# A decoder layer's attention stage: the tile pipeline rotated, the causal mask written in 32x32 tiles, the first exponentials issued earlier

## The reference, cut to what matters

```python
cq  = _layernorm(x @ W_dq, q_ln_w, q_ln_b)
Q   = cq @ W_uq ; Qr = rope(cq @ W_qr)            # 14 + 2 heads
ckv = _layernorm(x @ W_dkv, kv_ln_w, kv_ln_b)
Kn, V = split(ckv @ W_ukv) ; Kr = rope(x @ W_kr)
scores = einsum('bhqd,bhkd->bhqk', q, k) / sqrt(16)
scores = where(tril(ones(128, 128)), scores, -inf)
out = einsum('bhqk,bhkd->bhqd', softmax(scores), V) @ W_o.T
x1 = x + out                                      # then normalised for the cross attention
```

## Time and profile before

| | |
|---|---|
| time, median of 3 runs | 267.63 us (267.51 to 270.5) |
| span of the profiled execution, first to last instruction | 278.1 us |
| first scores (pass 0) to last scores (pass 7) | 25.80 to 110.47 us of that span |
| busy: TensorE, VectorE, ScalarE, GpSimd | 251.2, 152.3, 126.2, 90.9 us |
| mean granted TensorE clock | 0.974 |

### The profile page before, as it was taken

The page is one execution under the profiler, slowest core; times in us unless marked ns, Lnnn a source line. Parts: engine busy times, 40 slices in busy tenths (PEclk is TensorE's granted clock), DMA queues, the critical chain, the costliest instruction groups (busy, mean ns, idle before and its releaser), DMA issues.

```text
span 278.1 us, 4991 instructions
## 1 busy us (share of the span) xinstructions
PE 251.2 (90%) x1532; PEld 177.0 (64%) x1532; DVE 152.3 (55%) x460; ACT 126.2 (45%) x461; POOL 90.9 (33%) x106
## 2 busy tenths in 40 slices
PE   7789898999989899988798999899999777999993
PEld 6356566565556566766576787667777554776782
DVE  2344757878887875534889388653122212123174
ACT  1232959586685959850334314233341412334330
POOL 2110101121111110010554004656667575666550
PEclk9959999999999999999889999999999997999999
DMA  7999977300000620000002200223223232333494
GB/s 223 255 334 372 322 178 167 76 2 1 1 2 0 229 69 2 1 2 0 0 0 75 78 0 5 58 75 97 75 86 105 75 94 75 97 86 83 155 321 154
DMA packets 20851, 28.04 MB, mean 101 GB/s; under 512 B 2832, under 2 KB 17818, under 8 KB 20826
## 3 DMA queue, kind: packets, MB, share of 16 engines
q1 hardware_dynamic: 16683, 18.94, 22.7%
q0 software_dynamic: 2976, 8.13, 10.0%
q10 hardware_dynamic: 1167, 0.65, 0.9%
HBM read 21.55 MB, written 6.16 MB: 100 GB/s over the span
## 4 chain that ended last, share of the span: by engine, by line
PE 65%; DVE 9%; DMA 7%; ACT 6%; issue 5%; another core or an unknown queue 4%; POOL 2%; SPq 1%; ACTq 1%; DVEq 0%
PE bank L881 10%; PE bank L893 7%; PE bank L812 6%; PE bank L509 5%; PE bank L550 5%; ACT pr_s L990 4%; DMA lnkv_s<-in_ln_kv 4%; PE bank L540 3%; PE bank L825 3%; PE bank L562 3%; PE bank L585 3%; DMA x_s<-expert_out 2%; PE bank L862 2%; PE bank L531 2%
## 5 line engine op out<-in xcount | busy, mean ns | idle before, releaser
L990 ACT ACTIVATE pr_s<-bank,mx 128x128 f32<-128x128 f32 x128 | 46.6, 421 | 2.5 <-DVE mx L1213 2.5
L881 PE MATMUL bank<-gu_s,bxT 128*128 x124 | 42.9, 471 | 0.2 <-issue 0.2
L1533 DVE TENSOR_TENSOR pr_s<-bank,pr_s 128x176 f32<-128x176 f32 x31 | 10.6, 341 | 58.2 <-ACT pr_s L1152 39.9
L980 ACT ACTIVATE prT<-bank 128x512 f32<-128x512 f32 (+1 forms) x63 | 32.8, 521 | 15.0 <-PE bank L550 11.2
L467 POOL DMA_INDIRECT expert_out<-by,prT x31 | 30.8, 993 | 23.6 <-ACT by L980 14.9
L893 PE MATMUL bank<-dn_s,prT 88*128 x124 | 32.6, 387 | 3.0 <-issue 1.6
L462 POOL DMA_INDIRECT qx_s<-ffn_in,prT x31 | 30.1, 972 | 14.6 <-issue 8.9
L990 ACT ACTIVATION_READ_ACCUMULATOR pr_s<-bank,mx 128x1 f32 x128 | 33.6, 262 | 0.0
L881 PEld LDWEIGHTS bank<-gu_s,bxT 128*128 128x128 f32 x124 | 21.4, 192 | 8.0 <-issue 1.2
L893 PEld LDWEIGHTS bank<-dn_s,prT 88*128 88x128 f32 x124 | 21.8, 194 | 5.8 <-issue 3.4
L980 ACT ACTIVATE by<-bank 128x256 f32<-128x256 f32 x31 | 11.9, 384 | 27.4 <-PE bank L893 18.3
(11 more groups left out here) (188 smaller groups left out, 433.7 us busy)
## 6 DMA issues: line engine op xcount, KB each, us to landing
gu_s<-in_w_gu SPq DMA_DIRECT2D x8, 704.0 KB, 8.9
dn_s<-in_w_dn SPq DMA_DIRECT2D x4, 704.0 KB
qx_s<-in_ctx_in SPq DMA_DIRECT2D x2, 512.0 KB, 10.0
ffn_in<-x_s SPq DMA_DIRECT2D x4, 256.0 KB, 2.5
cv_s<-expert_out SPq DMA_DIRECT2D x4, 256.0 KB
x_s<-expert_out SPq DMA_DIRECT2D x4, 256.0 KB
out<-x_s SPq DMA_DIRECT2D x7, 128.0 KB
gu_s<-in_x_t SPq DMA_DIRECT2D x1, 768.0 KB, 11.4
```

The costliest lines, as they stand in the source:

```text
L881: last = mm(bank[2 + i % 2][:, 0:2 * I], bxT[:, i % 2, k, :], gu_s[:, k, bass.ds(e, 1), :], start=k == 0, stop=k == KD - 1)
L980: copy = lambda o, i: nc.scalar.activation(o, i, ACT.Copy)
L990: last = nc.scalar.activation(pr_s[:, n % 2, h, :], score_bank(n)[:, h * T:(h + 1) * T], ACT.Exp, bias=mx[:, n % 4, h:h + 1], accum_out=de ...
```

## The change

- **The mask.** The table of -1e30 becomes four tables (one for each quarter of the query rows), tabb grows from 96 KB to 192 KB. For every tile four matmuls of 128x128 weights and 512 columns become sixteen of 32x32 weights and 512 columns, four for each bank: the one at rows 32r and output partitions 32j. They stand together, right ahead of `scores(i)`, and wait for all four chunks' exponentials of the tile before. In the old order masks 0 and 1 stood behind `qk_transpose(i+1)`, mask 2 behind `weigh_values(n+1)`, mask 3 ahead of scores.
- **The rotation on TensorE.** `keys_values` and `queries` leave the end of the pass (tile i+2) and stand behind the scores (tile i+1): `queries(i+1)`, then `prob_transpose(n-1)`, `rden_transpose(i-1)`, then `keys_values(i+1)`, ahead of `front_project(i+2)`. Those of tile 1 leave the stretch ahead of the loop. The wait for the latents moves from `keys_values` to `queries`, and VectorE's `latents_out` waits for `keys_values` where it waited for `queries`. `cross_transpose` writes the upper half of bank 3 in place of bank 4 and waits for `dve_x1` or `act_x1_T`; `keys_values(b)` waits for `act_x1_T` from b = 4 on. In pass 0 the context keys stand behind `front_project(2)` and a block of context values behind `prob_transpose(1)`.
- **ScalarE.** `exps(n)` comes first in the pass, then `prT_out(n-1)`, then `kv_out(i+1)`.
- **VectorE.** The first `row_max` comes ahead of `q_out(i+1)`; x1's variance ahead of `latents_out`. The variance of x of tiles 2 to 7 is taken at once ahead of the loop, and GpSimd takes its powers there, in an instruction of their own; the latents' power has 2 columns in place of 3.

```diff
-    c = np.concatenate([np.where(p[None, :] <= p[:, None], 0.0, MASKED), p[:, None] < p[None, :], np.eye(128)], 1)
+    quarter = [np.where(p[None, :] <= 32 * j + p[:, None] % 32, 0.0, MASKED) for j in range(4)]
+    c = np.concatenate([p[:, None] < p[None, :], np.eye(128)] + quarter, 1)
...
-        tabb = sb("tabb", [128, 3 * 128], bf16)
-        maskb, trib, idb = (tabb[:, i * 128:(i + 1) * 128] for i in range(3))
+        tabb = sb("tabb", [128, 6 * 128], bf16)
+        trib, idb = (tabb[:, i * 128:(i + 1) * 128] for i in range(2))
+        maskq = tabb[:, 2 * 128:].rearrange("p (j k) -> p j k", j=4)
...
-        x1T_bank = lambda b: bank[4 if b < B - 4 else 3 if b < B - 1 else 0]
+        x1T_out_bank = lambda b: bank[3][:, D:2 * D] if b < B - 1 else bank[0][:, 0:D]
...
+            def rsqrt_x(n, lo, hi):
+                pool.wait_ge(dve_x_var, n)
+                nc.gpsimd.tensor_tensor(rsx[:, lo:hi], vex[:, lo:hi], halfpow[:, lo:hi], ALU.pow).then_inc(pool_x_rstd, 1)
...
+            rsqrt_x(1, 0, 1)
             rsqrt_latent(0)
+            rsqrt_x(2, 1, 2)
             rsqrt_latent(1)
+            rsqrt_x(3, 2, B)
...
             def keys_values(b):
-                pe.wait_ge(act_latents, b + 1) if b < 2 else pe.wait_ge(dve_latents, b - 1)
                 if b == 1:
                     pe.wait_ge(act_keys_values, 1)
                 if b == 2:
                     pe.wait_ge(act_ctx_values, 3)
                 if b >= 3:
                     pe.wait_ge(dve_x1, b - 2)
+                if b >= 4:
+                    pe.wait_ge(act_x1_T, b - 3)
                 for k in range(2):
                     last = mm(bank[3][:, 0:NOPE + D], ckvT[:, b % 2, k, :], wkv_s[:, k, :], start=k == 0, stop=k == 1)
                 last.then_inc(pe_keys_values, 1)
 
             def queries(b):
-                if b >= 4:
-                    pe.wait_ge(act_x1_T, b - 3)
+                pe.wait_ge(act_latents, b + 1) if b < 2 else pe.wait_ge(dve_latents, b - 1)
...
-            def mask(b, r):
+            def masks(b):
                 if b:
-                    pe.wait_ge(act_exp, NC * (b - 1) + r + 1)
-                mm(score_bank(r)[:].rearrange("p (h k) -> p h k", h=CH), idb, maskb.unsqueeze(1).to_broadcast([128, CH, T]),
-                   start=True, stop=False, skip_group_check=True)
+                    pe.wait_ge(act_exp, NC * b)
+                for r in range(NC):
+                    rows = slice(32 * r, 32 * r + 32)
+                    for j in range(4):
+                        mm(score_bank(r)[32 * j:32 * j + 32, :].rearrange("p (h k) -> p h k", h=CH), idb[rows, rows],
+                           maskq[rows, j:j + 1, :].to_broadcast([32, CH, T]), start=True, stop=False, skip_group_check=True)
...
-                if b < B - 4:
-                    pe.wait_ge(dve_latents, b + 3)
-                if b == B - 4:
+                if b < B - 3:
                     pe.wait_ge(dve_x1, b + 2)
-                if b == B - 3:
+                if b >= B - 3:
                     pe.wait_ge(act_x1_T, b)
                 for k in range(KD):
-                    last = tr(x1T_bank(b)[:, k * T:(k + 1) * T], xb[:, b % 2, k * 128:(k + 1) * 128], idf)
+                    last = tr(x1T_out_bank(b)[:, k * T:(k + 1) * T], xb[:, b % 2, k * 128:(k + 1) * 128], idf)
...
+            queries(0)
             keys_values(0)
-            queries(0)
             latent_transpose(1)
             ctx_values(0, 0)
             qk_transpose(0)
             ctx_values(0, 1)
-            keys_values(1)
-            queries(1)
             pe.wait_ge(ld_table_b, 16)
-            mask(0, 0)
             pe.wait_ge(act_ctx_values, 2)
-            mask(0, 1)
-            mask(0, 2)
             pe.wait_ge(dve_qk_T, 1)
 
             for i in range(B):
                 n = NC * i
-                mask(i, 3)
+                masks(i)
                 scores(i)
-                if i == B - 1:
-                    cross_transpose(i - 2)
+                if tiles(i + 1):
+                    queries(i + 1)
                 if tiles(i - 1):
                     prob_transpose(n - 1)
                     rden_transpose(i - 1)
+                if tiles(i + 1):
+                    keys_values(i + 1)
                 if i == B - 2:
                     pe.wait_ge(ld_wg_wo, 48)
                     gates(0, 0)
                     gates(0, 1)
+                if tiles(i + 2):
+                    front_project(i + 2)
                 if i == 0:
                     ctx_keys(1, 0)
                     ctx_keys(1, 1)
-                if tiles(i + 2):
-                    front_project(i + 2)
                 if i == 1:
                     ctx_values(1, 1)
                 if i == B - 1:
+                    cross_transpose(i - 2)
                     gates(1, 0)
                     gates(1, 1)
                 prob_transpose(n)
@@ -707,27 +718,20 @@
                     gates(2, 1)
                 if tiles(i + 1):
                     qk_transpose(i + 1)
-                    mask(i + 1, 0)
-                    mask(i + 1, 1)
                 prob_transpose(n + 1)
+                if i == 0:
+                    ctx_values(1, 0)
                 if i == 1:
                     pe.wait_ge(ld_w_out, 16)
                 if tiles(i - 1):
                     out_project(i - 1)
                 if tiles(i + 2):
                     latent_transpose(i + 2)
-                if i == 0:
-                    ctx_values(1, 0)
                 prob_transpose(n + 2)
                 weigh_values(n)
                 weigh_values(n + 1)
-                if tiles(i + 1):
-                    mask(i + 1, 2)
                 if tiles(i - 2) and i < B - 1:
                     cross_transpose(i - 2)
-                if tiles(i + 2):
-                    keys_values(i + 2)
-                    queries(i + 2)
...
+                exps(n)
+                if tiles(i - 1):
+                    prT_out(n - 1)
                 if tiles(i + 1):
                     kv_out(i + 1)
-                if i == B - 1:
-                    x1T_out(i - 2)
-                if tiles(i - 1):
-                    prT_out(n - 1)
-                exps(n)
                 if i == 0:
                     ctx_keys_out(1, 0)
                     ctx_keys_out(1, 1)
                 if i == 1:
                     ctx_values_out(1, 1)
+                if i == B - 1:
+                    x1T_out(i - 2)
                 if tiles(i - 1):
                     rdT_out(i - 1)
                 exps(n + 1)
                 prT_out(n)
                 exps(n + 2)
                 prT_out(n + 1)
-                exps(n + 3)
                 if i == 0:
                     ctx_values_out(1, 0)
+                exps(n + 3)
...
+            def x_variances(lo, hi):
+                dve.wait_ge(ld_x[xpart(lo)], 16)
+                for b in range(lo, hi):
+                    last = V.bn_stats(stx[:, b, :], x_s[:, b, :])
+                link(last)
+                for b in range(lo, hi):
+                    last = V.bn_aggr(agx[:, b, :], stx[:, b, :])
+                link(last)
+                V.tensor_scalar_add(vex[:, lo:hi], agx[:, lo:hi, 1], LN_EPS).then_inc(dve_x_var, 1)
...
             qk_out(0)
-            x_variance(2)
+            x_variances(2, B)
             tiles = lambda b: 0 <= b < B
 
             for i in range(B):
                 if tiles(i - 1):
                     denominators(i - 1)
+                row_max(NC * i)
                 if tiles(i + 1):
                     q_out(i + 1)
-                for r in range(NC):
+                for r in range(1, NC):
                     row_max(NC * i + r)
                 if i == 0:
                     dve.wait_ge(ld_ln, 32)
@@ -1345,13 +1361,11 @@
                     latent_normalize(i + 2)
                 if tiles(i - 1):
                     residual_attention(i - 1)
+                    x1_variance(i - 1)
                 if tiles(i + 2):
                     latents_out(i + 2)
                 if tiles(i - 1):
-                    x1_variance(i - 1)
                     x1_normalize(i - 1)
-                if tiles(i + 3):
-                    x_variance(i + 3)
```

More of the change, by code:

```diff
@@ L123, in decoder_layer @@
         tabr = wm_s[:].rearrange("p k n -> p (k n)")[:, 0:R_N]
-        tabb = sb("tabb", [128, 3 * 128], bf16)
-        maskb, trib, idb = (tabb[:, i * 128:(i + 1) * 128] for i in range(3))
+        tabb = sb("tabb", [128, 6 * 128], bf16)
+        trib, idb = (tabb[:, i * 128:(i + 1) * 128] for i in range(2))
+        maskq = tabb[:, 2 * 128:].rearrange("p (j k) -> p j k", j=4)
         onesb = sb("onesb", [128, 128], bf16)
-        halfpow = sb("halfpow", [128, 3])
+        halfpow = sb("halfpow", [128, B])
         wq_s = sb("wq_s", [128, QW])
@@ L174, in decoder_layer @@
         st = sb("st", [128, 2, 6])
+        stx, agx = sb("stx", [128, B, 6]), sb("agx", [128, B, 2])
         ag = sb("ag", [128, 2, 2, 2])
@@ L181, in decoder_layer @@
```

(25 more changed lines are left out.)

2 lines of the change are left out of this document (1 added, 1 removed).

## The result

The changed kernel takes 263.86 us (median of 17 runs), the kernel before in the same runs 267.81 us. The ratio is 0.9866, 95% interval 0.9843 to 0.9889: 3.6 us less (3.0 to 4.2). Both medians take in slower executions with a lower granted clock, and the ratio compares the others alone. I had forecast 1.1 us less. The time lies inside the range and the sign is right, but the gain is three times what my sum gave.

The account below looks back on a forecast made before the run. TensorE's waits and work were taken to bound the attention stage. Start -0.7, passes 2 to 5 -2.4 and pass 6 +2.0 sum to -1.1 us: from 267.63 to 266.5 us, range 262.5 to 270.5.

Parts of the forecast that it names:

- the price M of the mask block: Sixteen mask tiles' first start to scores: 0.8 us, from 36 ns each plus 0.2 for shape changes; bounds 0.4 and 1.06.
- The start: Ahead of the loop and passes 0 and 1: first scores 1.4 us earlier, 0.7 given back, so -0.7 us.
- the first (M = 1.2): Rival: sixteen masks cost what four did and the start gives back all 1.4 us; +2.8, 270.4 us, chance 0.20.
- the third (tiles of the same rows in line, 3.0 us): Rival: mask tiles reading the same rows can't run abreast, thirteen streams in line; +16.5, 284 us, chance 0.09.
- the second (everything folds): Rival: mask block costs 0.4 us and the stop ahead of `out_project` stays away; -7.8, 259.8 us, chance 0.13.
- the stop of 0.81 us: TensorE's wait ahead of `prob_transpose(n)` for the first exponentials; keys, values and queries cover it, saving 0.81 us a pass.
- The pair behind the q and k turn: Two masks behind `qk_transpose`: removal saves zero, as `out_project` waits 1.93 us from that turn for VectorE's turned keys.
- three of ScalarE's times within the pass: After the start of scores: first exponentials from 1.9 us, `kv_out` from 4.1, second exponentials from 4.9.
- the tie at the second turn: ScalarE's copy slot and TensorE both ready for `prob_transpose(n+1)` at 6.75 us, so any slip is a wait.
- the slack that I gave them: Fourth exponentials end at 9.97 us after scores start, masks waiting for them come at 10.94: ready by 1 us.
- mask 2 (0.29 us): Removing the wide mask behind `weigh_values(n+1)` was counted as a gain of 0.29 us a pass.
- the variance's way out of the loop: Taking x's variance out of VectorE's loop was costed at nothing, as TensorE doesn't wait for it in a pass.

Follow-up runs that it names:

- experiment 3: Changed kernel with the sixteen 32x32 tiles replaced by four 128x128 masks in the same place; ratio to before 1.0041, steady pass 11.91 us.
- experiment 5: Changed kernel with the block of sixteen mask tiles issued twice, one behind the other; ratio to before 0.9948, pass 11.62 or 11.63 us.
- experiment 6: Changed kernel with the tiles' two loops swapped, so neighbours take different rows; ratio to before 0.993, passes 11.41 or 11.42 us.
- experiment 2: Kernel before with only its four wide masks replaced by the sixteen-tile block ahead of scores, all orders old; ratio 1.0044, pass 12.49 us.
- 7: Changed kernel with ScalarE copying the last turned chunk ahead of the first exponentials again; ratio to before 0.987, steady passes 11.41 or 11.42 us.
- 4: Changed kernel with two more wide masks, only load, behind the q and k turn; ratio to before 0.9863, steady passes 11.41 or 11.42 us.
- 8: Changed kernel with the variance of x tile by tile in the loop again, on VectorE and GpSimd; ratio to before 0.991.
- best: Changed kernel with value matmuls moved ahead of `out_project` from pass 1, and pass 0's second exponentials ahead of the context keys' copies; ratio to before 0.980.

## Why the prediction was right in its mechanism and wrong in its size

**The failed step is the price M of the mask block.** I took 0.8 us, from a pace of 36 ns a matmul and two changes of shape. From its first start to scores it is 0.37 us, below even the 0.4 that I gave as bound and as a sign of being wrong; the change into the block falls ahead of its first start and costs the turn there 0.08 to 0.11 us (0.36, against 0.28 in experiment 3 and 0.25 in the earlier trace rows), which makes 0.45 to 0.48. Sixteen more tiles cost 0.21 us (experiment 5), 13 ns each, the time of one wide mask, so all sixteen run abreast. The 36 ns of the value matmuls is not a pace of issue, as I had read it: they are float32 with 128x32 weights, two instructions each, and at most four of them fit abreast. An estimate from the earlier trace rows: four float32 instructions of 256 columns in `out_project` last 1.10 us, 0.14 for 128 columns, and sixteen of these four abreast are 0.55 us, where 0.57 was measured. No run tests this reading of the 36 ns by itself.

With 0.47 for 0.8 a steady pass is 12.35 - 0.81 - 0.60 + 0.47 = 11.41 us, as measured. The sum names M in six places. The start came 0.4 us better than forecast, passes 2 to 5 1.3 in all and pass 6 0.4: 2.1 of the 2.3 us between my -1.1 and the -3.4 of the traces. The last 0.2 is in passes 0 and 1, where I had given back 0.7 without a term for M, so that the +0.48 measured there came near it by luck; the range and the rivals counted M eight times.

Of the rivals, the first (M = 1.2) is excluded by the trace, and the third (tiles of the same rows in line, 3.0 us) by the 0.37 us and by experiments 5 and 6. Of the second (everything folds) one half came true, M = 0.4; the other didn't, as the turned keys are as late as before.

The Trainium skill, "TensorE: Matmul & The Clock Gate", section on packing small matmuls, gives 660 ns for sixteen such tiles, run in parallel. That they run abreast the runs here confirm. But here the row of such a block lasts 0.43 us and the next group starts 0.37 behind its start; the measurement decides.

**Right, and tested:** the stop of 0.81 us goes because keys, values and queries cover it. It stays with the block in the old order (2), and in the new one it is gone with wide masks (3) and with ScalarE's old order (7); the swap on ScalarE alone in the old order was not run. The pair behind the q and k turn is free, 1.93 us from turn to `out_project` in every variant with that order (2, 4 and the changed kernel). The three of ScalarE's times within the pass that stand above were right to 0.05 us, the tie at the second turn became a wait of 0.15, and the fourth exponentials have the slack that I gave them in the steady passes. Passes 0 and 1 gave back 0.48 us, where I had 0.7.

**Half right:** I counted mask 2 (0.29 us) as a gain of its own. In the old order it covered a wait for the latents, as experiment 2 shows; the rotation takes that wait away, and the passes fit a gain of 0.29 there. And I costed the variance's way out of the loop at nothing, by asking what TensorE waits for in the old order. In the new one `rden_transpose` waits if the spread denominators slip, and with the variance back in the loop and GpSimd's power of x as an instruction of its own a pass takes 0.2 to 0.6 us more (8). The sum was not wrong by that, as the work is gone, but the reason doesn't carry over to the new order.

**The start** gave 1.8 us where I had 1.4 less a part given back; the 0.4 is again M. That the first row maximum waits for the six variances (to 24.10 in the first profile, where scores were done at 23.5) costs 0.17 us of pass 0 (8), little, since ScalarE then stands waiting 1.22 us for the context keys.

## What to carry to other kernels

Work that stands in another wait is free to keep and worthless to remove; before counting a removal, look for the wait that it covers, once in the old order and once in the new. Two parts of a change can each lose (here +0.4% and +0.4%) and gain together (-1.3%), so that testing parts one by one could have thrown away both. But look at what such a test moves besides: the second one here took the new order and left the masks in the place made for the small tiles, and the estimate with two of them back in their old, free place says that the order gains by itself. And where the nearest row differs in type from the new operation, ask first what sets its pace; here it was, by the estimate above, the float32 streams, four abreast, and not the count of instructions.

## What was not expected of the hardware

Sixteen 32x32 tiles of bfloat16 weights with 512 columns each take the time of one wide matmul of 512 columns: 0.21 us for a further block of sixteen (experiment 5), where a wide mask takes 0.215. Two orders of the tiles gave the same 0.37 us (experiment 6). The change from 128x128 to 32x32 costs the group ahead of it about 0.1 us (0.36 against 0.28).

TensorE's granted clock in the stretch from 15 to 20 us differed between executions of the same kernel: 0.50 and 1.00 in the two profiles of before, 0.68 and 0.59 in those of the changed kernel, and 1.00 in seven variants of it. Where it was 1.00 from there on, the new order with tiles reached its first scores at 20.8 to 21.5 us, and at 22.3 to 24.9 where it was lower. Of the 3.46 us between the first two profiles about half, 1.67, come with it. What decides it in one execution stays open. TensorE's busy time just before doesn't tell: it was 2.22 us of the stretch from 10 to 15 in the second profile of the changed kernel, which then fell to 0.59, and 2.17 in `best`, which stayed at 1.00.
